# Wider reads for the gate matmuls and the running sum of a linear attention stage

## The reference, cut to what matters

```python
# linear attention, H = 16 heads of 16 features
g = jax.nn.sigmoid(x.reshape(B, L, H, d) @ gw.T)
log_c = jnp.clip(jnp.cumsum(jnp.log(g), axis=1), -30.0, 30.0)   # running sum over the 256 tokens
Gc = (jnp.exp(log_c) + 1e-06)[..., None]
S = jnp.cumsum(KV * R / Gc, axis=1) * Gc
# gates of the mLSTM attention, 8 heads, an input and a forget gate: 16 columns
gate_in = jnp.concatenate([q, k, v], axis=-1)
ig = gate_in @ igate_w.T + igate_b
fg = gate_in @ fgate_w.T + fgate_b
```

## Time and profile before

| what | value |
|---|---|
| device time, median of 3 runs | 823.42 us |
| span of the profiled execution | 861.2 us |
| TensorE matmul busy | 768.0 us (89%) |
| TensorE weight load busy | 680.7 us (79%) |
| VectorE, ScalarE, GpSimd busy | 408.7, 347.6, 439.7 us |

### The profile page before, as it was taken

How to read it: one execution, slowest core, us unless ns; L and a number is a source line. 1 busy time by engine, 2 the same in 40 slices (tenths; PEclk the granted TensorE clock), 3 DMA queues, 4 the chain that set the end, 5 groups by cost and what they waited for, 6 DMA issues and landing times. The chain is left out here.

```text
span 861.2 us, 17237 instructions
## 1 busy us (share of the span) xinstructions
PE 768.0 (89%) x5882; PEld 680.7 (79%) x5883; DVE 408.7 (47%) x962; ACT 347.6 (40%) x874; POOL 439.7 (51%) x512
## 2 busy tenths in 40 slices
PE   7899999979498888898797887999999999999993
PEld 4677777769498787898687776689999999999992
DVE  3465555675334422323279998823333333333330
ACT  1343333344324323333376754144444444444430
POOL 5565665576667666666255542024444444444441
PEclk8999889999789999899889999999999999999997
DMA  8233333332332353233488799322222222122221
GB/s 285 75 101 98 105 104 105 93 110 84 87 91 86 102 162 91 85 89 86 121 227 213 187 274 351 137 81 37 37 37 37 37 35 37 33 37 35 37 31 18
DMA packets 75286, 87.78 MB, mean 102 GB/s; under 512 B 11936, under 2 KB 65504, under 8 KB 75104
## 3 DMA queue, kind: packets, MB, share of 16 engines
q0 software_dynamic: 19824, 43.93, 20.8%
q1 hardware_dynamic: 51728, 39.59, 16.1%
q10 hardware_dynamic: 3680, 3.54, 1.2%
HBM read 75.57 MB, written 11.47 MB: 101 GB/s over the span
## 5 line engine op out<-in xcount | busy, mean ns | idle before, releaser
L302 POOL DMA_INDIRECT G<-in_rpe,hopi x227 | 221.0, 974 | 132.6 <-issue 46.0
L1860 ACT ACTIVATE G<-ps,U 128x128 f32<-128x128 f32 x312 | 84.9, 383 | 161.0 <-PE ps L1808 161.0
L1808 PEld LDWEIGHTS ps<-G,QT 128*128 128x128 f32 x1248 | 145.2, 192 | 1.9
L1808 PE MATMUL ps<-G,QT 128*128 128x128 f32 x1248 | 145.5, 275 | 0.0
L1817 PE MATMUL ps<-G 128*128 x624 | 141.5, 380 | 1.2 <-DVE G L2004 1.2
L1817 PEld LDWEIGHTS ps<-G 128*128 128x128 f32 x624 | 115.5, 190 | 15.9 <-issue 1.6
L1055 PE MATMUL ps<-U,PET 128*128 128x128 f32 (+3 forms) x768 | 114.0, 292 | 11.0 <-issue 9.1
L1055 PEld LDWEIGHTS ps<-U,PET 128*128 128x128 f32 x768 | 104.9, 209 | 13.9 <-issue 13.4
L930 DVE COPY PET<-ps 128x512 f32<-128x512 f32 x64 | 43.8, 687 | 136.4 <-PE ps L983 53.4
L983 PE MATMUL ps<-cst,G 128*128 128x128 f32 x454 | 74.9, 288 | 18.4 <-issue 10.4
L1762 POOL DMA_INDIRECT out<-G,slots x39 | 67.4, 1728 | 22.3 <-issue 22.3
(11 more groups left out here) (243 smaller groups left out, 1201.5 us busy)
## 6 DMA issues: line engine op xcount, KB each, us to landing
G<-run_max SPq DMA_DIRECT2D x16, 512.0 KB, 8.0
U<-in_w SPq DMA_DIRECT2D x16, 512.0 KB, 7.4
G<-in_w SPq DMA_DIRECT2D x8, 1024.0 KB, 10.9
G<-in_rpe,hopi POOLq DMA_INDIRECT x227
U<-in_ctx SPq DMA_DIRECT2D x8, 256.0 KB
hidden_rows<-QT ACTq DMA_DIRECT2D x8, 256.0 KB, 7.4
out<-X SPq DMA_DIRECT2D x1, 2048.0 KB, 9.8
tokens_kept<-X SPq DMA_DIRECT2D x7, 256.0 KB
```

Of the source, the lines that this page charges most:

```text
L302: pool.indirect_dma_start(out=dst, out_offset=None, in_=rpe_d, in_offset=bass.IndirectOffsetOnAxis(ap=hopi[:, n:n + 1], axis=0)) \
L1808: mm = pe.matmul(bank(1 + 2 * u + c // 4, 4, P)[:, c % 4], w1c[u][:, k, c], hT[u][:, k, :], start=(k == 0), stop=(k == KC - 1))
L1860: ins = nc.scalar.activation(gel[u][:, c, :], bank(1 + 2 * u + c // 4, 4, P)[:, c % 4], ACT.Gelu, bias=b1c[u][:, c:c + 1])
```

## The change

The gates' 16 weight columns are read eight times over by each matmul, and 8 equal copies of each gate are written; VectorE reads the first copy. The running sum is made by two matmuls in place of three: the triangle times both tiles at once, with each tile's 16 columns read four times over, and then all ones times the first tile, read four times over, added to the second. VectorE's clamp reads the first copy. Waits, semaphores and the order of the work are as before.

```diff
+        NRC, NRG = 4, 8
 def cum(b):
-                o = bank(7, 2, HA)
-                pe.matmul(o[:, 0, :], tri, lgg[b % 2][:, 0, :], start=True, stop=True)
-                pe.matmul(o[:, 1, :], ones, lgg[b % 2][:, 0, :], start=True, stop=False)
-                pe.matmul(o[:, 1, :], tri, lgg[b % 2][:, 1, :], start=False, stop=True).then_inc(cum_full, 1)
+                o = bank(7, 2, NRC, HA)
+                pe.matmul(o, tri, lgg[b % 2].unsqueeze(2).to_broadcast([P, 2, NRC, HA]), start=True, stop=False)
+                pe.matmul(o[:, 1], ones, lgg[b % 2][:, 0:1, :].to_broadcast([P, NRC, HA]), start=False, stop=True) \
+                    .then_inc(cum_full, 1)
 def gates(b):
-                o = bank(5 if b < B - 1 else 3, 2, 2 * HX)
+                o = bank(5 if b < B - 1 else 3, 2, NRG, 2 * HX)
+
+                def w(k):
+                    return wg6[:, k:k + 1, :].to_broadcast([P, NRG, 2 * HX])
+
                 for c in range(2):
                     for k in range(KC):
-                        pe.matmul(o[:, c, :], cxT[:, k, c * P:(c + 1) * P], wg6[:, 2 + k, :],
+                        pe.matmul(o[:, c], cxT[:, k, c * P:(c + 1) * P], w(2 + k),
                                   start=(k == 0), stop=False)
                     for k in range(KC):
-                        mm = pe.matmul(o[:, c, :], QT[:, k, b, c * P:(c + 1) * P], wg6[:, k, :],
+                        mm = pe.matmul(o[:, c], QT[:, k, b, c * P:(c + 1) * P], w(k),
                                        start=False, stop=(k == KC - 1))
 VectorE:
-                    ins = nc.vector.tensor_tensor(o, bank(5 if b < B - 1 else 3, 2, 2 * HX)[:, c, :].unsqueeze(2), gbias.unsqueeze(2), ALU.add)
+                    ins = nc.vector.tensor_tensor(o, bank(5 if b < B - 1 else 3, 2, NRG, 2 * HX)[:, c, 0, :].unsqueeze(2), gbias.unsqueeze(2), ALU.add)
-                    clamp(gc[(b + 1) % 2], bank(7, 2, HA), cum_full, b + 2, cl_r)
+                    clamp(gc[(b + 1) % 2], bank(7, 2, NRC, HA)[:, :, 0, :], cum_full, b + 2, cl_r)
```

## The result

The changed kernel takes 818.92 us (median of 7 runs, 817.38 to 822.45), beside 823.35 us for the kernel before (7 runs, 820.09 to 824.79): ratio 0.9944, with a 95% interval of 0.9922 to 0.9966. It is faster by 4.4 us, half of the 8.8 us forecast. That lies inside the range of 809 to 822 us, but outside the forecast's own part of it, 809 to 817.4. In the experiments one of e4's 12 runs took 847.7 us at a lower clock, and its ratio leaves that run out.

A forecast was written before the change was run, and what follows sets the result against it. TensorE's own work, slowed by clock falls, was taken to bound the token stage, then a products chain starting at its handover. Savings 5.6 + 1.4 + 1.0 + 0.8 = 8.8 us off 823.42 gave 814.6 us; range 809 to 822, forecast's own 809 to 817.4.

The forecast's parts named there:

- rival C: GpSimd's gathers absorb the gain at the handover to the position products, leaving 820.2 us; chance 0.15.
- the clock of 1.00: Sign of being right: full granted clock in the stretches behind the gates of iterations 3 to 6.
- an iteration near 19 us: Sign of being right: a token-stage iteration near 19 us, against 20.54 us in the profile read.
- a first gather 7 to 9 us before 201.37: Sign of being right: the position products' first gather is issued that much earlier than in the profile read.
- (1): Gate matmuls read 128 columns in place of 16: +0.08 us a batch, +0.6 us for 8.
- (2): Running sum in two matmuls instead of three: -0.20 us a batch on TensorE's path, -1.6 us for 8.
- (3): VectorE's reads of these banks, the clamp's now strided: priced at nothing, up to 0.1 us a batch.
- (4): The clock fall behind the gates goes in iterations 3 to 6: 4 x 1.4 = 5.6 us saved.
- (5): The clock fall behind the last gates, at the first position products, goes: 1.4 us saved.
- (6): Low clock at the head of iteration 1, behind a running sum without gates, partly goes: 0.8 us saved.
- Rival A: The fall moves behind a longer TensorE wait at the state matmuls; slower, 826.4 us; chance 0.08.
- Rival B: The falls have another cause, such as transposes or scores, and stay; 822.4 us; chance 0.13.

The follow-up runs named there:

- e4: The kernel before with only the running sum changed to two matmuls reading their columns four times, gates still narrow, on the fast chip: 819.29 us, ratio 0.9946.
- e3: The kernel before with only the gates widened (columns read eight times), running sum as before, on the fast chip: 819.71 us, ratio 0.9948.
- e1: The kernel before, unchanged, profiled again on the fast chip: profiled execution 821.35 us.
- e8: The kernel before, unchanged, profiled once more on the second, slower chip: 869.66 us.
- e11: The changed kernel plus six additions (4.08 us) on GpSimd before its last token-stage gathers, third chip: 867.32 us, ratio 1.0030 to the kernel before.
- e12: The kernel before plus the same six additions (4.08 us) on GpSimd, third chip: 868.46 us, ratio 1.0024 to the kernel before.
- e9: The changed kernel as it is, on the third, slow chip: 864.68 us, ratio 0.9975 to the kernel before.
- e5: The kernel before with its narrow gate matmuls made twice over, second chip: 886.12 us, ratio 1.0167 to the kernel before.
- e6: The changed kernel with its wide gate matmuls made twice over, second chip: 877.30 us, ratio 1.0071 to the kernel before.
- e7: The changed kernel with the gates' columns read sixteen times, 256 per matmul, second chip: 877.81 us, ratio 1.0064 to the kernel before.

## Why the prediction was right, and where it was not

The direction, the cause and the way of the gain to the end were right; the size was twice too large. The time lay inside the range because the range reached to 822 us, for rival C's sake; the forecast's own part ended at 817.4. There was some luck in it: the count of falls came from the profile of a slower chip, and on such a chip the falls in the middle iterations turned out to cost next to nothing. Of the signs, the clock of 1.00, the 16 gate records in 1.78 us and the earlier end of the products' stage came true; an iteration near 19 us and a first gather 7 to 9 us before 201.37 can't be held against a fast chip's trace (18.13 us, 180.06). Step by step:

- **(1) Gates, +0.08 us a batch.** Right for the records: 1.78 against 1.71 us. The neighbouring row of the same width gave the price. The two shorter iterations at the end grew by more, 0.34 us together, and it is the wide gates that do it: e3 has them with the old sum and takes 13.67 and 11.42 us, e4 has the narrow ones with the new sum and takes 13.39 and 11.32, as e1 does.
- **(2) Running sum, -0.20 us a batch.** This term of 1.0 us net was mis-sized. The records are indeed fewer, but from the key transposes ahead of the gates to the token transposes behind the sum it is 95.90 - 93.25 = 2.65 us in e1 and 95.17 - 92.49 = 2.68 us after, and iterations without a fall are equally long (18.14 and 18.13). The step that failed here is "on TensorE's path". By the kernel's list of waits the transposes (`tokens_turned`) wait for VectorE to have read the gates, because both use bank 5. After the change VectorE's two reads of the gates end at 94.75 + 0.27 = 95.02, and the transposes start at 95.17, 0.15 us later:

```profile
94.75 0.27 DVE L828 TENSOR_TENSOR GT<-ps,U 128x16 f32<-128x16 f32 x2
```

  e3 and e4 bear this out. With the gates wide and the old sum (e3) the transposes start 2.40 us behind the first gates, as after the change; with the gates narrow and the new sum (e4) VectorE's reads end 0.10 us earlier and the transposes start at 2.31, again 0.15 us behind the reads. In e1 TensorE's own records last until 2.38. So the work saved in the sum becomes a wait whose end the gates set.
- **(3) VectorE's strided read, nothing.** Right: no full iteration without a fall became longer by more than 0.01 us, and e4, which has the clamp's strided read and not the wide gates, has the two short ones at e1's length.
- **(4) The clock in the token stage, 4 x 1.4 = 5.6 us.** This is the term that was most off, in its count and not in its price. A fall costs 1.20 and 1.39 us on the fast chip. But its trace held two such falls, not four. The count came from a profile in which every one of four iterations fell (and e8 repeats it); its iteration of 20.5 us is that of a slower chip, and the forecast was made for 823.42 us. On the slower chip itself the price was wrong: what the fall costs there had to be waited for anyway (e11 against e12), which neither the 0.54 nor the 1.51 us of the prediction allowed. With 2.60 us for this term, 1.65 for (5), nothing for (2), 0.34 lost to (1) and the 0.75 of the start, which isn't the change's, the sum is 4.66.
- **(5) The last gates, 1.4 us.** Right: 1.65 us from the last gates to gather 116, of which the first products alone make 1.71 - 0.89 = 0.82.
- **(6) The head of iteration 1, 0.8 us.** It wasn't there to be saved: e1 is at 1.00 from 20 to 95 us. On the slow chips it comes and goes, in e11 with the wide sum too (43 us, behind a wait of 1.02), so narrow columns aren't needed for it.
- **Rival A** (0.08) did not hold for the measured comparison but is real on the slow chip, where TensorE waits 2.37 us, longer than the 1.93 us of the earlier trace rows. It came behind three of five such waits in e9 and behind none of four in e11, so it is not the rule that the prediction made of it, and it doesn't turn the gain round: 0.9975, not slower.
- **Rival B** (0.13) fell with e5 and e6.
- **Rival C** (0.15): on the fast chip the handover still waits for TensorE, by 1.34 us instead of 3.02, and of the 4.66 us gained there 4.48 arrive at the last gather. On the slow chip e11 and e12 leave it open.

The Trainium skill (TensorE: Matmul & The Clock Gate, Why this matters for your kernels) asks that TensorE be kept busy without long idle gaps. e5 against e6 goes against the letter of it: the kernel that keeps TensorE busy for 171.56 of 180 us has a granted clock of 0.89, the one with 161.87 us has 1.00. Part 4 of the same page (PE-mode transpose) lets one expect that the transposes on both sides keep the clock from rising, which would have been rival B; they stayed, and the falls behind the gates went on all three chips (after, e6, e9). Falls behind idle time, which the page speaks of, are in e9, behind three of five waits of 2.37 us; that e11 has none behind waits as long shows that the length of the wait alone doesn't decide it.

Open: what holds VectorE and ScalarE up on the two slow chips; why the traces of slow chips have a fall behind five or six of the eight gates and the fast one's behind three, and whether it is the place of the narrow run in time that matters; whether the gates alone would do, since 0.9948 and 0.9937 can't be told apart; and how e7 stands to the changed kernel on the same chip.

## What to carry to other kernels

A run of matmuls with very few columns can cost more behind it than in it: look at the granted clock of the stretch that follows, and if it falls without an idle gap, read the few columns several times over, up to a width at which a record's spacing has hardly grown (128 here; 256 was too wide, and nothing between was run). Before multiplying the price of such a fall by a count, make sure that the profile is of a chip as fast as the one whose time is forecast: both the count of falls and their price differed between chips (three falls against six or seven, 1.2 to 1.4 us against next to nothing). And where an engine is made faster, ask what the next instruction waits for: a saving of 0.2 us just ahead of a wait was worth nothing.

## What the hardware showed that was not expected

- The same kernel takes 823, 866 or 872 us by chip. On the slow ones VectorE goes on 2 to 2.6 us late at the masks of the first scores, and ScalarE at the same moment (109.30 and 109.36 in e9), while the durations of the instructions are the same (1.15 us for the scores, 2.35 for the masks). That one hold-up makes an iteration of 20.5 us out of one of 18.1.
- The clock falls in the middle of a gapless run of narrow matmuls (107.03 in e5). In one trace each, a run of 1.71 us (e4) was followed by fewer falls than one of 2.38 us, and one of 0.66 us (e3) by none.
- A repeated read of 128 columns is taken at 0.111 us a record, of 16 at 0.107 and of 256 at 0.216.
